# Attention with a routed feed-forward layer on one core: the second head's sums of exponentials folded in two key tiles instead of one, and the denominator's small steps three key tiles later

## What is computed

```python
xn = layernorm(x)                           # x: 1 x 2048 x 128, float32
q, k, v = xn @ Wq, xn @ Wk, xn @ Wv         # 16 heads of 64
attn = softmax(q @ k.T * 64 ** -0.5)        # 2048 x 2048 for each head
out  = (attn @ v) @ Wo + bo
expert = argmax(softmax(xn @ router_w.T))   # one of 8 for each token
ffn  = (relu(xn @ fc[expert]) ** 2) @ proj[expert].T
result = x + out + ffn
```

## Time and profile before

| | us |
|---|---|
| median of 3 runs | 1335.16 (1334.42 to 1336.8) |
| the profiled execution's own time | 1333.57 |
| its span, first to last instruction | 1331.8 |
| TensorE busy | 1322.7 (99%) |
| VectorE busy | 1191.3 (89%) |
| GpSimd busy | 1128.2 (85%) |
| ScalarE busy | 708.3 (53%) |

### The profile page before, as it was taken

One profiled execution on the slowest core, in us unless ns is written; L12 is line 12 of the kernel. 1 busy time (PEld: TensorE's weight loads), 2 busy tenths in 40 slices (PEclk: granted clock), 3 DMA queues, 4 the chain that ended last, 5 costly groups with the idle time before them and its releaser, 6 DMA issues.

```text
span 1331.8 us, 20385 instructions
## 1 busy us (share of the span) xinstructions
PE 1322.7 (99%) x6338; PEld 867.1 (65%) x6338; DVE 1191.3 (89%) x1882; ACT 708.3 (53%) x1231; POOL 1128.2 (85%) x892
## 2 busy tenths in 40 slices
PE   8999999999999999999999999999999999999998
PEld 6765566766667766677666676666776666765554
DVE  7999999889888898898988989888998889989997
ACT  5654445654446644466544565444664445654453
POOL 7899999877888878798787988878988779888998
PEclk9999999999999999999999999999999999999999
DMA  5242212241123411233112432123311234011101
GB/s 143 55 106 71 67 44 56 63 102 48 43 58 78 100 35 42 59 93 85 42 43 50 102 77 52 34 58 93 93 35 35 66 78 100 11 37 42 35 17 40
DMA packets 85869, 82.78 MB, mean 62 GB/s; under 512 B 24513, under 2 KB 54913, under 8 KB 85761
## 3 DMA queue, kind: packets, MB, share of 16 engines
q1 hardware_dynamic: 84736, 79.38, 24.0%
q0 software_dynamic: 1024, 2.10, 0.6%
HBM read 27.00 MB, written 6.29 MB: 25 GB/s over the span
## 4 chain that ended last, share of the span: by engine, by line
PE 96%; DVE 2%; POOL 1%; issue 0%; DMA 0%; ACT 0%; DVEq 0%; ACTq 0%; POOLq 0%
PE OB L1231 33%; PE SB L1174 17%; PE MB L1202 17%; PE SB L1183 17%; PE XB L1259 2%; PE XB L1269 2%; PE XB L1155 2%; PE XB L1162 2%; DVE mx L827 1%; PE XB L1238 1%; PE XB L1239 1%; PE XB L1240 1%; POOL ex L592 0%; PE OB L1137 0%; DVE rd L992 0%
## 5 line engine op out<-in xcount | busy, mean ns | idle before, releaser
L558 POOL TENSOR_TENSOR acc<-acc,ex 128x512 f32<-128x512 f32 x690 | 911.5, 1348 | 29.1 <-ACT ex L698 1.1
L827 DVE TENSOR_REDUCE mx<-MB 128x1 f32<-128x512 f32 x992 | 639.4, 682 | 60.7 <-PE MB L1202 60.2
L698 ACT ACTIVATE ex<-SB 128x512 f32<-128x512 f32 x1024 | 607.8, 598 | 95.0 <-PE SB L1183 30.2
L1231 PE MATMUL OB<-ex,V 128*64 128x512 f32 x2048 | 447.2, 594 | 0.0
L1174 PE MATMUL SB<-Q,K 128*128 128x512 f32 x1024 | 410.0, 401 | 0.3 <-ACT ex L698 0.2
L1183 PE MATMUL SB<-Q,K 128*128 128x512 f32 x1024 | 399.3, 390 | 0.0
L1202 PE MATMUL MB<-K,Q 128*128 128x512 f32 x992 | 390.0, 394 | 1.0 <-DVE mx L827 0.7
L1231 PEld LDWEIGHTS OB<-ex,V 128*64 128x64 f32 x2048 | 144.0, 137 | 277.8 <-issue 274.2
L863 DVE TENSOR_TENSOR acc<-acc,ex 128x512 f32<-128x512 f32 x206 | 294.1, 1428 | 20.4 <-POOL acc L558 1.0
L726 ACT ACTIVATE osb<-OB 128x512 f32<-128x512 f32 x32 | 19.1, 597 | 449.1 <-PE OB L1231 449.1
L1174 PEld LDWEIGHTS SB<-Q,K 128*128 128x128 f32 x1024 | 192.5, 188 | 67.2 <-issue 27.6
(11 more groups left out here) (156 smaller groups left out, 637.2 us busy)
## 6 DMA issues: line engine op xcount, KB each, us to landing
Q<-high SPq DMA_DIRECT2D x124, 128.0 KB
K<-high SPq DMA_DIRECT2D x112, 128.0 KB, 2.3
Q<-low SPq DMA_DIRECT2D x62, 128.0 KB
rd<-rows_rd SPq DMA_DIRECT2D x62, 128.0 KB
K<-low SPq DMA_DIRECT2D x56, 128.0 KB, 2.4
w<-fc SPq DMA_DIRECT2D x23, 256.0 KB, 2.7
w<-projT SPq DMA_DIRECT2D x23, 256.0 KB, 3.0
sorted_x<-res SPq DMA_DIRECT2D x1, 1472.0 KB, 7.1
```

The source lines that it names most:

```text
L558: pool.tensor_tensor(a[:, :], src[:, :], EX[h][kt][:, :], ALU.add).then_inc(done, 1)
L698: act.activation(EX[h][kt][:, :], SB[bank_of(n, 2 * kt + h)][:, :], ACT.Exp).then_inc(a_e[h], 1)
L827: dve.tensor_reduce(mx[:, m % 2, u:u + 1], MB[bank_of(m, i)][:, :], AX.X, ALU.max).then_inc(v_m, 1)
L1231: mm = pe.matmul(OB[own[h], :], V[:, k, own[h]], EX[h][k][:, :], start=(k == 0), stop=(k == NT - 1))
```

## The change

`fold_sums` gets an argument `halves`: its transposition (half 0) and its reduction (half 1) can be called apart. In blocks that follow a block of `LATE`, the transposition stands behind the maxima of key tile 1 and the reduction behind those of key tile 2, and the four small steps stand at key tiles 4, 5, 6 and 7 instead of 2, 3, 4 and 5. The waits stay with the instructions they belong to. Nothing else is touched: the other blocks fold and step as before, and GpSimd's `normalise` still stands ahead of the additions of key tile 6.

```diff
-                def fold_sums(n, h):
-                    wait(dve, sums[h][n % 2], added(n, NT - 1))
-                    if h == 0:
-                        wait(dve, g_on, n.times(1))
-                    else:
-                        wait(dve, v_part, n.times(2, 1))
-                    dve.transpose(turned[:, :], acc[h][n % 2][:, :]).then_inc(v_turn, 1)
-                    wait(dve, v_turn, n.times(2, h + 1))
-                    dve.tensor_reduce(part[:, ...], turned[:, :]..., AX.X, ALU.add).then_inc(v_part, 1)
+                def fold_sums(n, h, halves=(0, 1)):
+                    if 0 in halves:
+                        wait(dve, sums[h][n % 2], added(n, NT - 1))
+                        if h == 0:
+                            wait(dve, g_on, n.times(1))
+                        else:
+                            wait(dve, v_part, n.times(2, 1))
+                        dve.transpose(turned[:, :], acc[h][n % 2][:, :]).then_inc(v_turn, 1)
+                    if 1 in halves:
+                        wait(dve, v_turn, n.times(2, h + 1))
+                        dve.tensor_reduce(part[:, ...], turned[:, :]..., AX.X, ALU.add).then_inc(v_part, 1)
...
                             late = n.off - 1 in LATE
-                            if late and kt == 1:
-                                fold_sums(n - 1, 1)
-                            sum_parts(n - 1, kt - late)
+                            if late and kt in (1, 2):
+                                fold_sums(n - 1, 1, (kt - 1,))
+                            sum_parts(n - 1, kt - 3 * late)
```

More of the change, by code:

```diff
@@ L982, in low_k @@
                     dve.tensor_tensor(low[:, :], XB[:, :], high[:, :], ALU.subtract).then_inc(v_k, 1)
-                def fold_sums(n, h):
-                    wait(dve, sums[h][n % 2], added(n, NT - 1))
-                    if h == 0:
-                        wait(dve, g_on, n.times(1))
-                    else:
-                        wait(dve, v_part, n.times(2, 1))
-                    dve.transpose(turned[:, :], acc[h][n % 2][:, :]).then_inc(v_turn, 1)
-                    wait(dve, v_turn, n.times(2, h + 1))
-                    dve.tensor_reduce(part[:, h * QB // SQ:(h + 1) * QB // SQ], turned[:, :].rearrange("p (t k) -> p t k", k=SQ),
-                                      AX.X, ALU.add).then_inc(v_part, 1)
+                def fold_sums(n, h, halves=(0, 1)):
[8 more added lines that the diff above has]
+                        wait(dve, v_turn, n.times(2, h + 1))
+                        dve.tensor_reduce(part[:, h * QB // SQ:(h + 1) * QB // SQ], turned[:, :].rearrange("p (t k) -> p t k", k=SQ),
+                                          AX.X, ALU.add).then_inc(v_part, 1)
                 def sum_parts(n, step):
```

## The result

The changed kernel takes 1346.11 us in the median of 4 runs (1345.55 to 1346.98) against 1335.35 for the kernel before: ratio 1.0083, 95% interval [1.0071, 1.0095]. It is 10.8 us slower. The forecast was 1338.4, slower by 3.2; the sign was right, the size was not, and the time lies outside the forecast's range, 1333.4 to 1341.4.

The account below looks back on a forecast made before the run. TensorE was taken to bound the kernel, so only its stalls count. The terms -2.0 + 4.4 + 0.8 = +3.2 us gave 1338.4 us against the median of 1335.16, range 1333.4 to 1341.4.

Parts of the forecast that it names:

- What bounds the kernel: Whole kernel: TensorE is busy 99% of the span, so only time in which it stands still, or its causes, counts.
- Part 1: Fold in two tiles and later steps: 0.4 us gained in each of blocks 1, 2, 3, 29, 30; -2.0 us.
- Part 2: Blocks 1 and 2: keys' DMAs behind the later reciprocal on SP delay `high_q`; TensorE stalls 2.4 and 2.0, +4.4 us.
- Part 3: GpSimd: `normalise` waits for the later `rd`, delaying last sums and folds around blocks 3 to 5 and 30; +0.8 us.
- Rival C: Slower by more: GpSimd's delay is not absorbed and its last sums hold up folds; 1340.7 us, chance 0.12.
- A: Rival: keys land in time in blocks 1 and 2, only parts 1 and 3 are left; 1334.0 us, chance 0.16.
- B: Rival: the stall goes whole in five blocks and the keys are in time; -5.5, 1329.7 us, chance 0.06.
- D: Rival: nothing matters, what SP has behind is hidden and the lag returns in the same size; 1335.2 us, chance 0.04.

Follow-up runs that it names:

- the mended kernel: Changed kernel with GpSimd's `normalise` one key tile later in six blocks, queries at tile 14 instead of 12 in blocks 1 and 2: 1334.33 us, ratio 0.9997.

## Why the prediction was wrong

**What bounds the kernel: right up to the last block.** Only TensorE's stalls counted, and what the blocks 0 to 30 are longer is stalls of TensorE or TensorE at the lower clock. In the last block the bound passed to VectorE.

**Part 1, the fold and the steps: right where nothing else is in the way.** 0.4 us a block were forecast; blocks 3 and 29 gave 0.44 and 0.47. Blocks 1, 2 and 30 never showed it as a shorter block: in the mended kernel they are -0.07, -0.20 and +0.58, so the sum of 2.0 us for five blocks was not reached in any run. The reciprocal came 3.0 us later in block 1 (2.9 forecast) and 2.3 in block 3 (2.3). The split by itself gives nothing that shows; beside the late steps it adds 0.1 us a block.

**Part 2, the keys on SP: right in mechanism and nearly in size.** The last of the keys' DMAs is issued 6.0 us behind the store of the reciprocal in both profiles (101.07 against 95.03). `high_q` idles 3.49 and 2.52 us; less the 0.31 that it always idles, 3.2 and 2.2 against 2.5 and 2.2 forecast. The keys landed 3.0 us behind the start of their last issue in block 1, not 2.4; that issue alone took 1.26. The stalls forecast at 2.4 and 2.0 were 2.7 and 1.8. The Trainium skill (DMA: Bandwidth & Descriptors, Anatomy of one DMA) gives its fixed 2.0 us for DMAs that GpSimd issues, which the prediction did not say. The DMAs here are issued by SP, and the store of `row` took 1.40 again (95.03 to 96.43), so the prediction was right to go by the row.

**Part 3, GpSimd: the step that failed by its size.** "`normalise` needs `rd`, some 4.3 us behind the reciprocal" put the landing of the two DMAs at 2.3 us, the median of another transfer of as many bytes (K<-high); the page of the changed kernel gives 3.0 for `rd`. The blocks that waited show 5.1 to 6.0 from the reciprocal's end to the product (in block 29, 1239.66 to 1245.70), of which the issues are 2.5. The kernel before had shown no wait at 6.4, and I took the lack of idle time for 2 us of slack; it was 0.4 to 1.3. So GpSimd waited 1.85 in block 29, not 0.2 to 0.4, and 3.24 in block 4; in all 10.6 us where some 6 were forecast. Blocks 4, 5 and 30 and the end became 1.20 + 1.36 + 1.50 + 1.71 = 5.8 us longer where the terms were +0.2, +0.4 and -0.2. Rival C had this mechanism, and its upper bound was too low: it stopped at block 30. That the last block hangs on VectorE's chain of additions behind the last fold, which is little shorter than TensorE's own work there, wasn't seen at all.

**Left out: the clock, some 3.3 us.** The prediction had no term for it. In the first profile the fall is in block 0, where nothing changed, and one could put it down to chance; the second profile has none there and two behind the stalls for the keys. Each profile loses 3.2 to 3.4 us, and by the mean granted clock none of the nine runs was without such a loss. Falls behind long stalls of TensorE stand in three profiles: the second one of the changed kernel (two), the product two tiles later (four) and the small steps alone (three, the third at 1274.9 behind a stall of 2.2 us). In blocks 1 to 30 no profile has a fall without a long stall, 1.9 us before it at most. That a stall is enough is not shown: the run with the keys first had none, nor had the changed kernel's first profile and that of blocks 1 and 2 alone, which had both lost clock in block 0. Why, no run here settles. In the kernel before and the mended ones a fall in block 0 in some runs would account for most of their spread (1333.1 to 1337.5); single profiles show it, the unprofiled runs only by their mean clock.

So 3.2 forecast became 10.8: 0.5 more from the keys, 5.4 more from GpSimd's lag, some 3.2 from the clock, 0.1 less in blocks 3 and 29, and 1.4 less by the medians. The profiled execution of the kernel before was 1.8 us under its median, that of the changed kernel 0.3 under its own; losses of clock in block 0 in the other runs of the kernel before would explain it.

**The rivals.** A and B needed the keys in time; they weren't. D fell with them. With the waits taken away the kernel was level with the one before. That its 1334.33 is near A's 1334.0 confirms nothing: the product and the queries were moved too, and its interval includes no change.

## What to carry to other kernels

A small step moved later carries everything behind it: list its successors on each in-order queue up to the next engine that waits, and for each the time by which it was early, not whether it waited. Where a profile shows no wait, the slack is unknown until the landing is measured; take it as zero for the bad case, and follow an engine that works without a pause to the very end of the kernel. Where TensorE will stand still for some 2 us in a full stream, add a price for its clock to the bad case; here it was 1.7 us a fall, behind some of the stalls.

## What the runs showed of the hardware

The granted clock of TensorE fell from 1.00 to 0.50 for 3.4 us at or behind stalls of 1.6 to 3.1 us in a stream of matmuls that was otherwise nearly without a gap. Each fall costs some 1.7 us on top of the stall, an estimate: half of its length. Yet stalls of 2.4, 1.9 and 1.5 us in the profile of the kernel with the keys first (blocks 2, 4 and 3) brought none, nor did one of 1.9 us in block 29 of the kernel with the product two tiles later. Of the twelve profiled executions six had a fall in block 0 (3.4 or 6.8 us long), three had falls behind stalls, none had both, and three had neither; the fall at the very end, where TensorE has run out of work, stands in all twelve and is not counted.
